# Adjacency times features on one core: main groups of five row tiles in place of four

## The chip, the cores and the metric

The kernel runs on one core of a Trainium2 chip. The metric is the device time of one execution in microseconds; the kernel before takes 638.62 us (median of 3 runs, 638.38 to 640.05).

## The reference

`x` is 8192 x 64, `adj` is 8192 x 8192, both float32. What is computed:

```
agg = adj @ (x @ W_agg)
y   = w[:, None] * relu(agg) + (1 - w)[:, None] * x
out = layernorm(x + y)            # over the 64 columns, eps 1e-5, no scale or shift
```

The adjacency matrix is 268.4 MB and is read once; everything else is small.

## The kernel before

The product is taken in the order (adj @ x) @ W_agg. The 8192 nodes are 64 tiles of 128 rows of the output, and 64 tiles of 128 source nodes. An adjacency tile is stored transposed and packed on the host, so that one row of a load (one SBUF partition) holds, for a run of source tiles, the columns of several row tiles side by side. TensorE holds a tile of `x` (128 x 64) as weights and streams the adjacency; the 64 x columns sums are gathered in PSUM. Even source tiles write PSUM partitions 0 to 63, odd ones 64 to 127 (`into[j % 2 * D:...]`), so two neighbouring matmuls use different halves of the array. `aggT` then holds the sums of both halves, and a second matmul with `wagg2` (W_agg twice, one over the other) turns them into rows and adds the halves.

The row tiles come in three stages: main, 60 row tiles in G = 15 groups of `MAIN_SLOTS` = 4 (512 columns); mid, 3 row tiles (384 columns); last, 1 row tile (128 columns).

- Loads (SyncE, lines 105 to 137). A main group comes in three loads of `MAIN_LOADS` = 22, 22 and 20 source tiles; row c of the ring is a slot of 22 x 512 columns (44 KB in a partition, 132 KB for three). A load's rows are 45,056 or 40,960 bytes, 128 of them. Load c of the next group waits until TensorE has finished slot c (`slot_free`). Mid (8 loads, L130) and last (9 loads, L136) reuse the same ring behind the last main group. The rows 0 to 62 of the output tiles are stored by SyncE (L141) when mid is normalised, the last one by ScalarE (L214).
- TensorE (L144 to L187). In a hardware loop over the groups: for each load wait for `loaded[c]`, then `contract` (L156), one matmul for each source tile; the profile shows each float32 matmul as two records of LDWEIGHTS and two of MATMUL. Then `turn_back` (L164), four matmuls of 64 columns with 128 x 128 weights, behind the wait for ScalarE's copy. After the loop the same for mid and last, written out.
- ScalarE (L203) copies the sums of a group from PSUM into `aggT` when all three loads are contracted, and takes square roots (L199).
- VectorE (L230 to L267): relu, weight, residual and layer norm of a group from `rows_ps`, seven short steps.

One DMA queue (SyncE's) carries all loads in program order, and each engine's work is in program order too.

Of the kernel before, what the change touches and what calls it, by code (L numbers as in the profile page):

```python
# [4 lines left out]
P = 128  # L5
D = 64
EPS = 1e-5
HALVES = 1
MAIN_SLOTS = 4
MID_SLOTS = 3  # L10
LAST_SLOTS = 1
SUB = 64
MAIN_LOADS = (22, 22, 20)
# [4 lines left out]
def gnn_residual_layernorm(nc, x, adj_main, adj_mid, adj_last, w, w_agg, out):  # L18
# [15 lines left out]
    T = x.shape[0] // P  # L34
    G = adj_main.shape[0]
    MID, LAST = G, G + 1
    MID_T0 = G * MAIN_SLOTS
    LAST_T0 = MID_T0 + MID_SLOTS
    COLS, MID_COLS = MAIN_SLOTS * P, MID_SLOTS * P
    C = len(MAIN_LOADS)  # L40
    SLOT = max(MAIN_LOADS) * COLS
    LAST_AT = T * MID_COLS
    assert SUB == T == sum(MAIN_LOADS) == sum(MID_LOADS) == sum(LAST_LOADS) and LAST_T0 + LAST_SLOTS == T
    assert LAST_AT + T * P <= C * SLOT and LAST_AT > (C - 1) * SLOT


    DVE_PRE = 2
# [5 lines left out]
    with ctx:  # L53
        def sb(name, shape):
            return ctx.enter_context(nc.sbuf_tensor(name, shape, fp32))

        def psum(name, shape):
            return ctx.enter_context(nc.psum_tensor(name, shape, fp32))

        def sem(name):  # L60
            return ctx.enter_context(nc.semaphore(name))

        ring = sb("ring", [P, C * SLOT])
        x_sb = sb("x_sb", [P, T, D])
# [5 lines left out]
        aggT = sb("aggT", [P, COLS])  # L70
        y = sb("y", [P, MAIN_SLOTS, D])
        sq = sb("sq", [P, MAIN_SLOTS, D])
        rowsum = sb("rowsum", [P, MAIN_SLOTS])
        varsum = sb("varsum", [P, MAIN_SLOTS])
        std = sb("std", [P, MAIN_SLOTS])
# [5 lines left out]
        mv = sb("mv", [P, 2])  # L81

        bank = psum("bank", [P, 8, 512])
        acc = bank[:, 0]
        mid_acc = bank[:, 1, 0:MID_COLS]
        last_acc = bank[:, 2, 0:P]
        rows_ps = bank[:, 3, 0:MAIN_SLOTS * D]
        mid_rows = bank[:, 4, 0:MID_SLOTS * D]
        last_rows = bank[:, 5, 0:D]

        loaded = [sem(f"loaded{c}") for c in range(C)]
        mid_loaded = [sem(f"mid_loaded{k}") for k in range(len(MID_LOADS))]
# [1 line left out]
        slot_free = sem("slot_free")  # L94
# [3 lines left out]
        agg_copied = sem("agg_copied")  # L98
# [8 lines left out]
        @block.sync  # L107
        def _(sp):
            sp.dma_start(x_sb[:], x.rearrange("(p t) d -> p t d", p=P)).then_inc(x_in, 16)  # L109
            sp.dma_start(w_sb[:], w.rearrange("(p t) -> p t", p=P)).then_inc(w_in, 16)  # L110
            def main_load(c, load):

                j, n = sum(MAIN_LOADS[:c]), MAIN_LOADS[c]
                sp.dma_start(ring[:, c * SLOT:c * SLOT + n * COLS], load[:, :, j:j + n].rearrange("o q s n -> (o q) (s n)")  # L114
                             ).then_inc(loaded[c], 16)

            for c in range(C):
                main_load(c, adj_main[0:1, 0])
            with sp.Fori(1, G) as g:
                for c in range(C):  # L120

                    sp.wait_ge(slot_free, g * C + (c + 1 - C))
                    main_load(c, adj_main[bass.ds(g, 1), 0])

            j, freed = 0, 0
            for k, n in enumerate(MID_LOADS):
                while freed * SLOT < (j + n) * MID_COLS:
                    freed += 1
                    sp.wait_ge(slot_free, (G - 1) * C + freed)
                sp.dma_start(ring[:, j * MID_COLS:(j + n) * MID_COLS],  # L130
                             adj_mid[0, :, j:j + n].rearrange("q s n -> q (s n)")).then_inc(mid_loaded[k], 16)
                j += n
            sp.wait_ge(slot_free, G * C)
            j = 0
            for k, n in enumerate(LAST_LOADS):
                sp.dma_start(ring[:, LAST_AT + j * P:LAST_AT + (j + n) * P],  # L136
                             adj_last[:, j:j + n].rearrange("q s n -> q (s n)")).then_inc(last_loaded[k], 16)
                j += n

            sp.wait_ge(out_ready, LAST)  # L140
            sp.dma_start(out_rows[:, 0:LAST_T0], res[:, 0:LAST_T0]).then_inc(stored, 16)  # L141
# [5 lines left out]
        @block.tensor  # L147
        def _(pe):
            pe.wait_ge(x_in, 16)
            pe.wait_ge(wagg_in, 32)  # L150

            def contract(into, at, cols, j0, n):

                for s in range(n):
                    j = j0 + s
                    last = nc.tensor.matmul(into[j % 2 * D:(j % 2 + 1) * D, 0:cols], x_sb[:, j],  # L156
                                            ring[:, at + s * cols:at + (s + 1) * cols], start=j < 2, stop=j >= T - 2)
                return last

            def turn_back(rows, n, copied):  # L160

                pe.wait_ge(agg_copied, copied)
                for i in range(n):
                    last = nc.tensor.matmul(rows[:, i * D:(i + 1) * D], aggT[:, i * P:(i + 1) * P], wagg2[:], start=True, stop=True)  # L164
                last.then_inc(rows_done, 1)

            with pe.Fori(0, G) as g:
                for c in range(C):
                    pe.wait_ge(loaded[c], g * 16 + 16)
                    contract(acc, c * SLOT, COLS, sum(MAIN_LOADS[:c]), MAIN_LOADS[c]).then_inc(slot_free, 1)  # L170

                pe.wait_ge(dve_step, g * DVE_GROUP + DVE_PRE)
                turn_back(rows_ps, MAIN_SLOTS, g + 1)
            j = 0
            for k, n in enumerate(MID_LOADS):
                pe.wait_ge(mid_loaded[k], 16)
                last = contract(mid_acc, j * MID_COLS, MID_COLS, j, n)
                j += n
            last.then_inc(mid_done, 1)
            turn_back(mid_rows, MID_SLOTS, MID + 1)  # L180
            j = 0
            for k, n in enumerate(LAST_LOADS):
                pe.wait_ge(last_loaded[k], 16)
                last = contract(last_acc, LAST_AT + j * P, P, j, n)
                j += n
            last.then_inc(last_done, 1)
            turn_back(last_rows, LAST_SLOTS, LAST + 1)  # L187

        @block.scalar
        def _(act):  # L190
            for h in range(2):
                act.dma_start(wagg2[h * D:(h + 1) * D, :], w_agg).then_inc(wagg_in, 16)

            nc.scalar.preload_act_table_set("sqrt_and_others")  # L194
            act.wait_ge(eps_ready, 1)

            def std_of(out_std, var, scale, var_step):
                act.wait_ge(dve_step, var_step)
                nc.scalar.activation(out_std, var, ACT.Sqrt, bias=eps[:, 0:1], scale=scale).then_inc(std_ready, 1)  # L199

            with act.Fori(0, G) as g:
                act.wait_ge(slot_free, g * C + C)
                nc.scalar.copy(aggT[:], acc).then_inc(agg_copied, 1)  # L203
                std_of(std[:], varsum[:], 1.0 / D, g * DVE_GROUP + (DVE_PRE + VAR_STEP))

                act.wait_ge(out_ready, g + 1)
            act.wait_ge(mid_done, 1)
            nc.scalar.copy(aggT[:, 0:MID_COLS], mid_acc).then_inc(agg_copied, 1)  # L208
            std_of(std[:, 0:MID_SLOTS], varsum[:, 0:MID_SLOTS], 1.0 / D, MID * DVE_GROUP + (DVE_PRE + VAR_STEP))
            act.wait_ge(last_done, 1)  # L210
            nc.scalar.copy(aggT[:, 0:P], last_acc).then_inc(agg_copied, 1)  # L211
            std_of(std_last[:], mv[:, 1:2], 1.0, LAST_STEP0 + LAST_VAR_STEP)
            act.wait_ge(out_ready, LAST + 1)
            act.dma_start(out_rows[:, LAST_T0:T], res[:, LAST_T0:T]).then_inc(stored, 16)  # L214
            act.wait_ge(stored, 2 * 16)
# [85 lines left out]
```

## Time and profile before

| | before |
|---|---|
| time, median of 3 runs | 638.62 us (638.38 to 640.05) |
| time of the profiled execution | 638.89 us |
| its span, first to last instruction | 637.0 us |
| TensorE matmul busy | 519.5 us (82%) |
| VectorE busy | 55.8 us (9%) |
| ScalarE busy | 15.9 us (2%) |
| DMA queue of SyncE, share of 16 DMA engines | 99.6% |
| moved | 272.75 MB, mean 428 GB/s |
| mean granted TensorE clock | 0.912 |

The time of an execution is 1.9 us longer than its span. Busy times are unions: an engine with two operations at once counts once. "Idle before" is time in which an engine had nothing running, with what ended it.

### The profile page before, as it was taken

The page shows a single profiled execution, that of the slowest core. Times are in us where ns is not written, and L with a number is a line of the kernel's source. Part 1 is how long each engine was busy: PE and PEld are TensorE (multiplying, and loading weights), DVE is VectorE, ACT ScalarE, POOL GpSimd, SP SyncE. Part 2 cuts the span into 40 slices and gives each one's busy share as a digit, 9 for nine tenths or more (in the row PEclk, how much of TensorE's full clock was granted, in tenths as well). Part 3 has the DMA queues.
Part 4 walks back from the last instruction along what each step waited for, and adds up shares of the span by engine and source line. Part 5 has one row for each costly group of instructions (what it writes and reads, how often), then busy time and mean ns, then how long its engine had stood idle before and what let it go on. Part 6 is the DMA issues. An engine that isn't in the chain of part 4 may idle for free.

```text
span 637.0 us, 5371 instructions
## 1 busy us (share of the span) xinstructions
PE 519.5 (82%) x2304; PEld 177.2 (28%) x2304; DVE 55.8 (9%) x136; ACT 15.9 (2%) x35; POOL 0.3 (0%) x5
## 2 busy tenths in 40 slices
PE   0678798878987888797878977878887987978996
PEld 0123232222222322222222322322222222222345
DVE  2000101010010100101001010100101001010102
ACT  0000000000000000000000000000000000000000
POOL 0000000000000000000000000000000000000000
PEclk9997898888979889897988979898888989888999
DMA  9999999999999999999999999999999999999998
GB/s 362 453 418 453 419 427 433 425 447 428 444 414 447 419 429 443 441 432 419 451 410 436 436 450 423 427 431 425 446 424 453 424 429 419 436 444 420 428 413 349
DMA packets 9667, 272.75 MB, mean 428 GB/s; under 512 B 1472, under 2 KB 1728, under 8 KB 3008
## 3 DMA queue, kind: packets, MB, share of 16 engines
q1 hardware_dynamic: 9360, 272.63, 99.6%
q10 hardware_dynamic: 304, 0.07, 0.1%
q8 instruction: 3, 0.05, 0.0%
HBM read 270.60 MB, written 2.10 MB: 428 GB/s over the span
## 4 chain that ended last, share of the span: by engine, by line
DMA 69%; PE 29%; issue 0%; SPq 0%; ACT 0%; DVE 0%; DVEq 0%
DMA ring<-adj_main_dram 69%; PE bank L156 29%; PE bank L164 0%; SPq L114 0%; ACT aggT L203 0%; ACT aggT L208 0%; SPq L110 0%; SPq L109 0%; DVE res L267 0%; ACT std_last L199 0%; DVE y_last L261 0%; ACT aggT L211 0%; DVE stats L263 0%; DVE y_last L262 0%; DVE mv L264 0%
## 5 line engine op out<-in xcount | busy, mean ns | idle before, releaser
L156 PE MATMUL bank<-ring,x_sb 128*64 128x512 f32 (+2 forms) x2176 | 501.7, 621 | 102.2 <-DMA ring<-adj_main_dram 102.1
L156 PEld LDWEIGHTS bank<-ring,x_sb 128*64 128x64 f32 x2176 | 161.6, 148 | 430.2 <-issue 299.7
L245 DVE SCALAR_TENSOR_TENSOR y<-bank,w_sb 128x256 f32<-128x256 f32 (+1 forms) x16 | 6.7, 420 | 552.7 <-PE bank L164 552.7
L164 PE MATMUL bank<-wagg,aggT 128*128 128x64 f32 x128 | 17.9, 281 | 11.2 <-ACT aggT L203 10.3
L164 PEld LDWEIGHTS bank<-wagg,aggT 128*128 128x128 f32 x128 | 15.6, 191 | 25.4 <-ACT aggT L203 23.5
L203 ACT COPY aggT<-bank 128x512 f32<-128x512 f32 x15 | 8.8, 585 | 527.0 <-PE bank L156 527.0
L234 DVE TENSOR_TENSOR y<-y,res 128x256 f32<-128x256 f32 (+1 forms) x16 | 6.7, 420 | 2.2
L242 DVE TENSOR_TENSOR res<-y,rstd 128x256 f32 (+1 forms) x16 | 6.7, 421 | 0.6
L238 DVE TENSOR_TENSOR sq<-y 128x256 f32<-128x256 f32 (+1 forms) x16 | 6.7, 421 | 0.6
L236 DVE SCALAR_TENSOR_TENSOR y<-rowsum,y 128x256 f32<-128x256 f32 (+1 forms) x16 | 6.7, 420 | 0.5
L239 DVE TENSOR_REDUCE varsum<-sq 128x4 f32<-128x256 f32 (+1 forms) x16 | 6.7, 416 | 0.5
L235 DVE TENSOR_REDUCE rowsum<-y 128x4 f32<-128x256 f32 (+1 forms) x16 | 6.6, 416 | 0.6
L199 ACT ACTIVATE std<-varsum,eps 128x4 f32<-128x4 f32 (+1 forms) x16 | 4.8, 297 | 65.7 <-DVE varsum L239 65.7
L230 DVE TENSOR_TENSOR res<-x_sb,two_minus_w 128x4096 f32<-128x4096 f32 x1 | 4.4, 4425 | 0.0
L241 DVE RECIPROCAL rstd<-std 128x4 f32<-128x4 f32 (+1 forms) x16 | 2.8, 178 | 6.9 <-ACT std L199 6.9
L194 ACT ACT_TABLE_LOAD x1 | 1.3, 1283 | 2.0 <-issue 2.0
L227 DVE TENSOR_SCALAR two_minus_w<-w_sb 128x64 f32<-128x64 f32 x1 | 0.2, 194 | 9.2 <-DMA w_sb<-w_dram 9.2
L208 ACT COPY aggT<-bank 128x384 f32<-128x384 f32 x1 | 0.5, 478 | 17.5 <-PE bank L156 17.5
L261 DVE TENSOR_SCALAR y_last<-bank,w_sb 128x64 f32<-128x64 f32 x1 | 0.3, 284 | 4.8 <-PE bank L164 4.8
L211 ACT COPY aggT<-bank 128x128 f32<-128x128 f32 x1 | 0.3, 265 | 4.7 <-PE bank L156 4.7
L199 ACT ACTIVATE std_last<-mv,eps 128x1 f32<-128x1 f32 x1 | 0.3, 296 | 1.6 <-DVE mv L264 1.6
L267 DVE TENSOR_SCALAR res<-y_last,mv,rstd_last 128x64 f32<-128x64 f32 x1 | 0.3, 314 | 0.0
(9 smaller groups left out, 1.3 us busy)
## 6 DMA issues: line engine op xcount, KB each, us to landing
ring<-adj_main_dram SPq DMA_DIRECT2D x30, 5632.0 KB, 27.2
ring<-adj_main_dram SPq DMA_DIRECT2D x15, 5120.0 KB, 29.8
ring<-adj_mid_dram SPq DMA_DIRECT2D x2, 2304.0 KB, 22.8
ring<-adj_mid_dram SPq DMA_DIRECT2D x1, 3072.0 KB, 21.5
ring<-adj_mid_dram SPq DMA_DIRECT2D x2, 1536.0 KB, 23.9
x_sb<-x_dram SPq DMA_DIRECT2D x1, 2048.0 KB, 8.0
out_dram<-res SPq DMA_DIRECT2D x1, 2016.0 KB, 8.1
ring<-adj_last_dram SPq DMA_DIRECT2D x2, 768.0 KB, 23.0
```

What stands on the lines that cost most here:

```text
L156: last = nc.tensor.matmul(into[j % 2 * D:(j % 2 + 1) * D, 0:cols], x_sb[:, j], ring[:, at + s * cols:at + (s + 1) * cols], start=j < 2, st ...
L164: last = nc.tensor.matmul(rows[:, i * D:(i + 1) * D], aggT[:, i * P:(i + 1) * P], wagg2[:], start=True, stop=True)
L199: nc.scalar.activation(out_std, var, ACT.Sqrt, bias=eps[:, 0:1], scale=scale).then_inc(std_ready, 1)
L203: nc.scalar.copy(aggT[:], acc).then_inc(agg_copied, 1)
L230: step(nc.vector.tensor_tensor(res[:], x_sb[:], over_row(two_minus_w[:]), ALU.mult), DVE_PRE)
L234: step(nc.vector.tensor_tensor(v, v, residual, ALU.add), base + 2)
L235: step(nc.vector.tensor_reduce(rowsum[:, 0:n], v, AX.X, ALU.add), base + 3)
L236: step(nc.vector.scalar_tensor_tensor(out=v, in0=over_row(rowsum[:, 0:n]), scalar=-1.0 / D, in1=v, op0=ALU.mult, op1=ALU.add), base + 4)
L238: step(nc.vector.tensor_tensor(s, v, v, ALU.mult), base + 5)
L239: step(nc.vector.tensor_reduce(varsum[:, 0:n], s, AX.X, ALU.add), base + VAR_STEP)
L242: nc.vector.tensor_tensor(residual, v, over_row(rstd[:, 0:n]), ALU.mult).then_inc(out_ready, 1)
L245: step(nc.vector.scalar_tensor_tensor(out=y[:, 0:n], in0=rows.rearrange("p (n d) -> p n d", d=D), scalar=0.0, in1=over_row(w_sb[:, bass.ds ...
```

## The change

`MAIN_SLOTS` goes from 4 to 5: twelve main groups in place of fifteen, each of 640 columns. The source tiles of the three loads stay 22, 22 and 20, so the rows of a load grow to 56,320 and 51,200 bytes and the ring to 165 KB. 640 float32 columns do not fit one PSUM bank of 512, so the sums of a group lie in two (`acc` with 512 columns, `acc_rest` with 128), and each source tile takes two matmuls. They are issued for two source tiles at a time: even and odd tile into `acc`, then even and odd tile into `acc_rest`. ScalarE copies the two banks one after the other, and `turn_back` has five matmuls. Mid and last are as before, in other banks. The counts awaited on `agg_copied` follow from two copies in each group. The bytes moved and the multiply-adds are the same.

```diff
-MAIN_SLOTS = 4
+MAIN_SLOTS = 5
...
-    assert LAST_AT + T * P <= C * SLOT and LAST_AT > (C - 1) * SLOT
+    assert LAST_AT + T * P <= C * SLOT and all(n % 2 == 0 for n in MAIN_LOADS)
...
-        acc = bank[:, 0]
-        mid_acc = bank[:, 1, 0:MID_COLS]
-        last_acc = bank[:, 2, 0:P]
-        rows_ps = bank[:, 3, 0:MAIN_SLOTS * D]
-        mid_rows = bank[:, 4, 0:MID_SLOTS * D]
-        last_rows = bank[:, 5, 0:D]
+        BANK = bank.shape[2]
+        acc, acc_rest = bank[:, 0], bank[:, 1, 0:COLS - BANK]
+        mid_acc = bank[:, 2, 0:MID_COLS]
+        last_acc = bank[:, 3, 0:P]
+        rows_ps = bank[:, 4, 0:MAIN_SLOTS * D]
+        mid_rows = bank[:, 5, 0:MID_SLOTS * D]
+        last_rows = bank[:, 6, 0:D]
...
+            def contract_main(c):
+
+                for s in range(0, MAIN_LOADS[c], 2):
+                    for into, c0, c1 in (acc, 0, BANK), (acc_rest, BANK, COLS):
+                        for half in range(2):
+                            j, at = sum(MAIN_LOADS[:c]) + s + half, c * SLOT + (s + half) * COLS
+                            last = nc.tensor.matmul(into[half * D:(half + 1) * D], x_sb[:, j], ring[:, at + c0:at + c1],
+                                                    start=j < 2, stop=j >= T - 2)
+                return last
+
...
-                    contract(acc, c * SLOT, COLS, sum(MAIN_LOADS[:c]), MAIN_LOADS[c]).then_inc(slot_free, 1)
+                    contract_main(c).then_inc(slot_free, 1)
 
                 pe.wait_ge(dve_step, g * DVE_GROUP + DVE_PRE)
-                turn_back(rows_ps, MAIN_SLOTS, g + 1)
+                turn_back(rows_ps, MAIN_SLOTS, g * 2 + 2)
...
-                nc.scalar.copy(aggT[:], acc).then_inc(agg_copied, 1)
+                nc.scalar.copy(aggT[:, 0:BANK], acc).then_inc(agg_copied, 1)
+                nc.scalar.copy(aggT[:, BANK:COLS], acc_rest).then_inc(agg_copied, 1)
```

## Rows read from the trace of the kernel before

**Rows 1.** The page's DMA queues: packets, MB, share of the 16 engines' span.

```profile
q1 hardware_dynamic: 9360, 272.63, 99.6%
q8 instruction: 3, 0.05, 0.0%
```

**Rows 2.** TensorE's timeline, two groups: start us, us, operation, idle before and its end.

```profile
126.51 8.80 PE L156 MATMUL bank<-ring,x_sb 128*64 128x512 f32 x40 [0.76 <-DMA ring<-adj_main_dram]
136.00 1.10 PE L164 MATMUL bank<-wagg,aggT 128*128 128x64 f32 x8 [0.69 <-ACT aggT L203]
139.84 11.21 PE L156 MATMUL bank<-ring,x_sb 128*64 128x512 f32 x44 [2.73 <-DMA ring<-adj_main_dram]
153.18 11.36 PE L156 MATMUL bank<-ring,x_sb 128*64 128x512 f32 x44 [2.14 <-DMA ring<-adj_main_dram]
165.30 8.80 PE L156 MATMUL bank<-ring,x_sb 128*64 128x512 f32 x40 [0.76 <-DMA ring<-adj_main_dram]
```

**Rows 3.** The chain that ended last, from the last main load: start us, us, what.

```profile
562.14 29.77 DMA ring<-adj_main_dram
591.91 0.04 issue
591.95 8.83 PE bank L156 x40
600.78 0.02 issue
600.80 0.59 ACT aggT L203
...
602.55 20.82 PE bank L156 x128
```

**Rows 4.** TensorE's timeline, from the mid stage to the end.

```profile
623.92 0.88 PE L164 MATMUL bank<-wagg,aggT 128*128 128x64 f32 x6 [0.58 <-ACT aggT L208]
624.73 7.38 PE L156 MATMUL bank<-ring,x_sb 128*64 128x128 f32 x128
```

**Rows 5.** The issue of the smallest loads of the last stage, and the page's line for them.

```profile
617.46 0.79 SPq L136 DMA_DIRECT2D ring<-adj_last_dram  x1
...
ring<-adj_last_dram SPq DMA_DIRECT2D x2, 128.0 KB, 14.4
```

**Rows 6.** DMA totals from 100 to 560 us with the queue's line, and from 621 to 629.

```profile
DMA packets 5121, 199.17 MB, mean 433 GB/s; under 512 B 561, under 2 KB 561, under 8 KB 561
q1 hardware_dynamic: 5121, 199.17, 100.3%
...
DMA packets 937, 3.25 MB, mean 406 GB/s; under 512 B 100, under 2 KB 210, under 8 KB 937
```

**Rows 7.** TensorE's timeline, first microseconds of the last stage, and of last main load.

```profile
624.73 2.19 PE L156 MATMUL bank<-ring,x_sb 128*64 128x128 f32 x36
624.73 5.02 PE L156 MATMUL bank<-ring,x_sb 128*64 128x128 f32 x88
...
591.95 0.20 PEld L156 LDWEIGHTS bank<-ring,x_sb 128*64 128x64 f32 x4 [1.65 <-DMA ring<-adj_main_dram]
592.43 0.14 PEld L156 LDWEIGHTS bank<-ring,x_sb 128*64 128x64 f32 x2 [0.29 <-issue]
592.86 0.14 PEld L156 LDWEIGHTS bank<-ring,x_sb 128*64 128x64 f32 x2 [0.29 <-issue]
```

**Rows 8.** ScalarE's copy of 128 columns, by form: busy us, mean ns, idle before.

```profile
L211 ACT COPY aggT<-bank 128x128 f32<-128x128 f32 x1 | 0.3, 265 | 4.7 <-PE bank L156 4.7
```

**Rows 9.** TensorE's timeline, first group, and DMA queues from 42 to 47 us.

```profile
35.36 9.66 PE L156 MATMUL bank<-ring,x_sb 128*64 128x512 f32 x44 [1.25 <-DMA ring<-adj_main_dram]
48.95 11.41 PE L156 MATMUL bank<-ring,x_sb 128*64 128x512 f32 x40 [3.92 <-DMA ring<-adj_main_dram]
...
q1 hardware_dynamic: 75, 2.52, 117.4%
q8 instruction: 1, 0.02, 1.4%
```

**Rows 10.** Third loads: the chain; timeline; two stretches with busy us, granted clock, DMA share, GB/s.

```profile
126.51 8.83 PE bank L156 x40
...
514.38 10.53 PE bank L156 x40
...
204.09 10.50 PE L156 MATMUL bank<-ring,x_sb 128*64 128x512 f32 x40 [2.46 <-DMA ring<-adj_main_dram]
...
204.00:214.70 10.70, 10.50 (x40) 3.18 (x40) 0.84 0.94 404
591.90:600.80 8.90, 8.80 (x40) 2.78 (x40) 1.00 0.99 423
```

More of the change, by code:

```diff
@@ L179, in _ @@
             last.then_inc(mid_done, 1)
-            turn_back(mid_rows, MID_SLOTS, MID + 1)
+            turn_back(mid_rows, MID_SLOTS, G * 2 + 1)
             j = 0
@@ L186, in _ @@
             last.then_inc(last_done, 1)
-            turn_back(last_rows, LAST_SLOTS, LAST + 1)
+            turn_back(last_rows, LAST_SLOTS, G * 2 + 2)
         @block.scalar
```

## The prediction

> **What bounds the kernel now.** I read four views in this order. The page's DMA queues come first: SyncE's queue fills 99.6% of the 16 engines' span [rows 1]. So the stream of loads sets the pace, and a main group takes what its bytes take: the third loads of two neighbouring groups are met by TensorE at 126.51 and 165.30 us, 38.79 us apart [rows 2]. In TensorE's timeline every load of a group is waited for, with 0.76, 2.73 and 2.14 us of idle time [rows 2]. There TensorE has slack, and what it does more costs nothing as long as the slot comes free before the two other loads in the queue have landed; they last over 25 us, TensorE needs 9 to 12.
>
> The third view is the chain from the last main load on. It lands at 591.91 us, and from there the chain is TensorE without a wait for data: 8.83 us of contraction, ScalarE's copy of 0.59 us, `turn_back`, 20.82 us of mid [rows 3]. In this stretch the slack is gone, because mid and last carry fewer columns for each source tile and TensorE is about as slow as the stream. The fourth view, the timeline of the end, tells how near the two are. The last loads land at about 617.46 + 14.4 = 631.9 us [rows 5]; TensorE finishes at 624.73 + 7.38 = 632.11 [rows 4]. How long would it take if nothing held it? The first 36 records of the last stage take 2.19 us and the first 88 take 5.02 [rows 7]. They run two by two, so 26 pairs take 2.83 us, 0.109 us each, and the 20 pairs up to 128 records would take 2.18 more: 7.20 us. The row has 7.38. The data hold TensorE up by only 0.18 us: at the end of the kernel both bound it, within 0.2 us. Whatever makes TensorE later between the last main landing and the end shows up in full, and whatever makes the stream faster helps only through the landing of that last main load.
>
> **The change, part by part.**
>
> *The stream.* Bytes are the same, rows fewer: each of the 16 engines carries 8 of the 128 rows of a load, so 15 groups x 3 x 8 = 360 main rows become 12 x 3 x 8 = 288, 72 fewer. What a row costs beyond its bytes comes from two stretches [rows 6]. From 100 to 560 us: 5121 - 561 = 4560 rows, 43.7 KB each (199.17 MB by 4560), 460 us x 16 / 4560 = 1614 ns a row. From 621 to 629 us: 837 rows of 3.88 KB, 8 x 16 / 837 = 153 ns. The slope is 1461 ns for 39.8 KB, 36.7 ns a KB; what remains is 153 - 143 = 10 ns a row. 72 x 10 ns = 0.7 us less. Bounds: nothing, and 1.1 us were it 15 ns. I take -0.7 us for the landing of the last main load.
>
> *Contraction of the last main load.* 20 source tiles get a second matmul of 128 columns. The last stage shows just such matmuls at 0.109 us for a pair of records [rows 7]; 20 tiles have 40 records, 20 pairs: 20 x 0.109 = +2.2 us. Bounds: nothing (short steps wholly beside long ones, G below), and +5.4 (F below); I take the step of the row, since it is the same shape, back to back. In the same load the 512-column part stays at 8.8 us. In all other main loads the same kind of time (22 x 0.11 = 2.4 us) lies in the wait for the next load, which grows with it: a stream of 13.3 us for 44 KB rows becomes 16.7 us.
>
> *ScalarE.* A second copy, of 128 columns, behind the first: 0.265 us [rows 8] plus a little issue, +0.3 us. TensorE's `turn_back` waits for both, and mid is queued behind it.
>
> *turn_back.* 8 records take 1.10 us, 6 take 0.88 [rows 2, 4]; two more cost +0.22 us.
>
> *VectorE.* 320 columns in place of 256 in seven steps of a group; nobody waits for a main group's result before the store at the end, and mid's own steps are unchanged: nothing. *SyncE:* 9 loads fewer to issue, mid's loads are freed earlier; nothing, since the queue is full. Three fewer loop turns hide in TensorE's idle time.
>
> *Sum.* TensorE's path behind the last main landing grows by 2.2 + 0.3 + 0.22 = 2.7 us; the 0.18 us in which it was held up is used up by it: +2.5. The landing is 0.7 earlier: +1.8 us. The final store starts that much later as well. The profiled execution took 638.89 us, so 640.7 on its scale; it lies 0.27 us above the median of 638.62, so **640.4 us**. Its own range is 639.7 to 641.3 (the row cost from 1.1 to 0 us, and 0.1 or 0.2 us for the copy and the changes between shapes). A measurement of this kernel can tell about 0.3%, 1.9 us, from no change: the forecast is just below that.
>
> **The rivals.**
>
> *B, slower: the last main load meets the lower clock.* In 8 of the 13 third loads that stand by themselves in the chain TensorE needs 8.83 us, the first at 126.51, the last at 591.95 [rows 3, 10]; in 5 about 10.5 us, the first at 204.09, the last at 514.38 [rows 10]. At 204.09 the granted clock of the stretch is 0.84 in place of 1.00 [rows 10], part of it at 1.2 in place of 2.4 GHz. That one comes behind a longer idle time, 2.46 us against 0.76 for the fast ones shown [rows 2, 10]. With the change the second load takes 2.4 us more and the stream between second and third grows by 3.0, so the idle time is about 0.6 us longer: 1.4 or 3.1 us. The price is the 1.7 us of the rows, now fully on the path: 642.1 us. It decides as soon as the last third load starts at the low clock.
>
> *C, earlier: code.* Between 42 and 47 us one packet of instructions comes in (0.02 MB) [rows 9], and the third load of the first group takes 13.59 us from landing to landing (35.36 to 48.95) in place of the 12.12 of 153.18 to 165.30 [rows 2, 9]. 1.47 us are lost there on one DMA engine and never come back. The changed loop body has 64 more matmuls, so such packets come at other moments and perhaps on other engines. If none falls on the latest engine: 638.9 us. *D:* one more falls there: 641.9.
>
> *E: the loop body no longer stays in the instruction memory.* Between 100 and 560 us all 5121 packets are SyncE's loads [rows 6], none is code, though the loop turns 12 times. Were the larger body fetched anew at each of the 11 returns, and each time at 1.5 us on the deciding engine, it would be +16.5, 656.9 us. The Trainium skill (Runtime: NRT & Kernel Launch, Instruction fetch mechanics) has the rule that a taken branch out of a window of two 16 KiB pages forces a fetch, and gives TensorE 128 KiB of instruction memory; by the first this change would pay, by the second not. No row here shows a body of this size.
>
> *F: short and long matmuls don't pair.* Before, two records start together at every step, from the first weights of a load on (4 weight loads in 0.20 us, then 2 in every 0.43) [rows 7]. If records kept strict program order (both of the even tile, then both of the odd one), a pair of tiles would take three long steps and a short one, 3 x 0.43 + 0.11 = 1.40 us, in place of 2 x 0.43 + 2 x 0.11 = 1.08: +3.2 us over 10 pairs, 643.6. Against it speaks the common start of the first two. The Trainium skill (TensorE: Matmul & The Clock Gate, Part 3, The mechanism) says that matmuls start and end in program order; that rule would favour F.
>
> *G, faster: the stream alone decides.* If the short matmuls cost nearly nothing beside the long ones, the end follows the stream, -0.7 us, 637.9; with C, 636.4.
>
> **How the numbers follow.** Forecast 0.48 (within 0.3% 0.27, slower 0.21), B 0.20, C 0.12 (0.11 within, 0.01 faster), D 0.06, E 0.03, F 0.04, G 0.07 (0.03 within, 0.04 faster). Slower: 0.21 + 0.20 + 0.06 + 0.03 + 0.04 = 0.54. Within: 0.27 + 0.11 + 0.03 = 0.41. Faster: 0.05. The range 638.3 to 642.8 holds the forecast, B, C and D, 0.86 less their edges; E, F and G lie mostly outside.
>
> **What would show it.** In the changed profile: third loads 48.3 to 48.5 us apart (38.79 x 1.25 less 0.2); the last main load landing near 591.2 us and contracted in about 11.0 us; two ScalarE copies, 0.9 us together; mid starting near 604.3 in place of 602.5; mid at 20.8 us; the last stage without any wait, 7.2 us. B shows as a last contraction over 12.5 us, C and D as the landing moved by 1.5 us, E as instruction packets in every group, F as 14 us. The prediction is wrong if TensorE waits for data in the last stage again.

## The result and the profile after

The changed kernel takes 640.31 us (median of 16 runs, 639.81 to 642.02), the kernel before in runs beside it 639.15 us (16 runs, 638.38 to 640.27). The ratio is 1.0022 with a 95% interval of 1.0013 to 1.0031: 0.2% slower, less than the 0.3% that the prediction took as its bound. 640.4 us had been forecast.

The times of both kernels lie in two clusters. Before: 8 runs from 638.4 to 638.9 us and 8 from 639.4 to 640.3. After: 11 runs from 639.8 to 640.4 and 5 from 641.7 to 642.0. Lower cluster against lower cluster (638.75 and 640.22, their medians) the change costs 1.5 us. Both profiled executions are of the lower one.

| | before | after |
|---|---|---|
| profiled execution / span | 638.89 / 637.0 us | 640.43 / 638.5 us |
| TensorE matmul busy | 519.5 us | 508.7 us |
| last main load landed | 591.91 us | 591.22 us |
| its contraction | 8.83 us | 11.01 us |
| start of mid | 602.48 us | 604.36 us |
| last stage | 624.73 + 7.38 us | 626.61 + 7.21 us |

The queues of the changed kernel on its page (packets, MB, share of the 16 engines) are those of [rows 1] with 1296 packets fewer, and one more of instructions:

```profile
q1 hardware_dynamic: 8064, 272.63, 99.2%
q10 hardware_dynamic: 304, 0.07, 0.0%
q8 instruction: 4, 0.07, 0.0%
```

The chain of the changed kernel, two neighbouring third loads and then the stretch behind the last one (start us, us, what), answers to [rows 2, 3]:

```profile
494.37 0.04 issue
494.42 11.01 PE bank L167 x80
...
542.80 0.04 issue
542.84 12.70 PE bank L167 x80
...
591.22 0.04 issue
591.26 11.01 PE bank L167 x80
602.27 0.02 issue
602.29 0.04 ACT aggT L214
602.34 0.44 issue
602.78 0.28 ACT aggT L215
603.06 0.04 issue
603.10 1.33 PE bank L175 x10
604.43 20.82 PE bank L157 x128
```

Third loads land 48.43 us apart, 542.80 to 591.22 among them. From the last one on there is again no wait for data, and each piece of TensorE's path that the change touches is longer. The second copy (L215) begins at 602.78 us, 0.10 us before the first one (602.29 + 0.59) ends, so the chain shows only a part of the first. TensorE's timeline of the end, which answers to [rows 4], shows the last stage without its hold:

```profile
625.80 0.88 PE L175 MATMUL bank<-wagg,aggT 128*128 128x64 f32 x6 [0.58 <-ACT aggT L220]
626.61 7.21 PE L157 MATMUL bank<-ring,x_sb 128*64 128x128 f32 x128
```

### The profile page after: what moved, and what is told of

Same layout as the page of the kernel before. It is cut to its first block, busy times and chain, and to the rows that moved or that the text cites. A ratio compares the mean times of both kernels' runs of the same rounds, so it can differ in the third digit from the quotient of the medians.

```text
span 638.5 us, 7549 instructions
## 1 busy us (share of the span) xinstructions
PE 508.7 (80%) x3456; PEld 239.1 (37%) x3456; DVE 52.2 (8%) x112; ACT 15.3 (2%) x41; POOL 0.3 (0%) x5
## 4 chain that ended last, share of the span: by engine, by line
DMA 70%; PE 29%; issue 0%; SPq 0%; DVE 0%; ACT 0%; another core or an unknown queue 0%; DVEq 0%
DMA ring<-adj_main_dram 70%; PE bank L167 24%; PE bank L157 4%; PE bank L175 0%; SPq L115 0%; ACT aggT L220 0%; SPq L111 0%; SPq L110 0%; DVE res L279 0%; ACT std_last L210 0%; DVE y_last L273 0%; ACT aggT L215 0%; ACT aggT L223 0%; DVE stats L275 0%
## 5 line engine op out<-in xcount | busy, mean ns | idle before, releaser
L167 PE MATMUL bank<-ring,x_sb 128*64 128x512 f32 (+1 forms) x3072 | 463.5, 465 | 114.8 <-DMA ring<-adj_main_dram 114.8
L167 PEld LDWEIGHTS bank<-ring,x_sb 128*64 128x64 f32 x3072 | 207.7, 146 | 369.2 <-issue 247.1
L257 DVE SCALAR_TENSOR_TENSOR y<-bank,w_sb 128x320 f32<-128x320 f32 (+1 forms) x13 | 6.3, 481 | 560.3 <-PE bank L175 560.3
L157 PE MATMUL bank<-ring,x_sb 128*64 128x384 f32 (+1 forms) x256 | 28.1, 380 | 0.0
L157 PEld LDWEIGHTS bank<-ring,x_sb 128*64 128x64 f32 x256 | 16.1, 137 | 11.2 <-issue 11.1
L246 DVE TENSOR_TENSOR y<-y,res 128x320 f32<-128x320 f32 (+1 forms) x13 | 6.3, 482 | 1.7
L254 DVE TENSOR_TENSOR res<-y,rstd 128x320 f32 (+1 forms) x13 | 6.3, 483 | 0.4
L248 DVE SCALAR_TENSOR_TENSOR y<-rowsum,y 128x320 f32<-128x320 f32 (+1 forms) x13 | 6.3, 483 | 0.4
L250 DVE TENSOR_TENSOR sq<-y 128x320 f32<-128x320 f32 (+1 forms) x13 | 6.3, 481 | 0.4
L247 DVE TENSOR_REDUCE rowsum<-y 128x5 f32<-128x320 f32 (+1 forms) x13 | 6.2, 478 | 0.4
L251 DVE TENSOR_REDUCE varsum<-sq 128x5 f32<-128x320 f32 (+1 forms) x13 | 6.2, 477 | 0.4
L215 ACT COPY aggT<-bank 128x128 f32<-128x128 f32 x12 | 3.3, 271 | 0.0
```

The source lines that it names most:

```text
L167: last = nc.tensor.matmul(into[half * D:(half + 1) * D], x_sb[:, j], ring[:, at + c0:at + c1], start=j < 2, stop=j >= T - 2)
L246: step(nc.vector.tensor_tensor(v, v, residual, ALU.add), base + 2)
L247: step(nc.vector.tensor_reduce(rowsum[:, 0:n], v, AX.X, ALU.add), base + 3)
L248: step(nc.vector.scalar_tensor_tensor(out=v, in0=over_row(rowsum[:, 0:n]), scalar=-1.0 / D, in1=v, op0=ALU.mult, op1=ALU.add), base + 4)
L250: step(nc.vector.tensor_tensor(s, v, v, ALU.mult), base + 5)
L251: step(nc.vector.tensor_reduce(varsum[:, 0:n], s, AX.X, ALU.add), base + VAR_STEP)
```

## The experiments

**What sets the end.** Two theories stood: TensorE's work behind the last main landing, or something else that five row tiles bring with them (start-up, copies, queue). The first experiment leaves the 128-column matmuls of every third load out, all but those of its last pair of source tiles; a part of the sums is then missing.

```diff
-                    for into, c0, c1 in (acc, 0, BANK), (acc_rest, BANK, COLS):
+                    for into, c0, c1 in ((acc, 0, BANK), (acc_rest, BANK, COLS))[:1 if c == C - 1 and s < MAIN_LOADS[c] - 2 else 2]:
```

> The 128-column matmuls of the third load are left out in every group but for the last pair of source tiles, so that part of the sums of one row tile in five is missing. Theory (TensorE's work behind the last main landing sets the end): 9 pairs x 0.218 us = 2.0 us less there, lower cluster at 638.3 us (changed kernel 640.2 less 2.0, of which the data give back nothing since TensorE's end would be 631.9 us and the data allow 631.5). Rival (the 1.7 us come from something else: the start-up, the copies, the queue): no change, 640.2 us.

Measured: median 639.55 us over 10 runs, five from 638.35 to 638.85 and five from 640.24 to 640.62. On the same chip the changed kernel's lower cluster lay at 640.39 (below), 1.6 us higher, where 2.0 had been expected. TensorE's timeline of the third contraction and of the last stage:

```profile
591.13 9.02 PE L167 MATMUL bank<-ring,x_sb 128*64 128x512 f32 x44 [1.39 <-DMA ring<-adj_main_dram]
624.52 7.21 PE L157 MATMUL bank<-ring,x_sb 128*64 128x128 f32 x128
```

The contraction is 1.97 us shorter (10.99 less 9.02), the load is met within 0.2 us of the same time, and the last stage starts 2.09 us earlier than at 626.61, without a hold. So the work behind the landing does set the end of the changed kernel. The profiled execution (638.51 us) is 1.9 us below the first one of the changed kernel and 2.0 below the one of the same chip; the clusters' medians (638.81 and 640.39) differ by 0.4 less, and why is open. The upper cluster stays, at 640.43 us in five of ten runs.

**The two clusters.** Theory: in the upper one the last third load is contracted partly at 1.2 GHz, as some third loads of earlier groups are. Loads of 24, 22 and 18 source tiles shorten the third contraction, and the shorter stream between the second and the third load leaves less idle time before it; the ring is packed for it.

```diff
-MAIN_LOADS = (22, 22, 20)
+MAIN_LOADS = (24, 22, 18)
...
-    SLOT = max(MAIN_LOADS) * COLS
+    AT = [sum(MAIN_LOADS[:c]) * COLS for c in range(C + 1)]
...
-                sp.dma_start(ring[:, c * SLOT:c * SLOT + n * COLS], load[:, :, j:j + n].rearrange("o q s n -> (o q) (s n)")
+                sp.dma_start(ring[:, AT[c]:AT[c] + n * COLS], load[:, :, j:j + n].rearrange("o q s n -> (o q) (s n)")
```

> Loads of 24, 22 and 18 source tiles in place of 22, 22 and 20, packed without gaps in the ring; rows 61,440, 56,320 and 46,080 bytes, as many rows as before the edit. Theory: the third contraction has one pair less, 1.08 us, so the lower cluster falls from 640.2 to 639.1 us; and since the stream between second and third landing (13.6 us) is about as long as the second contraction (11.9 at full clock, 13.6 with its slow start), TensorE has at most 1.8 us idle before the third load and starts it at full clock: the upper cluster is gone. Rival (the clusters don't come from the clock): the upper cluster stays at +1.7 us in a third of the runs.

Measured: 639.14 us, ten runs from 638.87 to 639.47, 1.25 us below the lower cluster of the changed kernel on the same chip (1.1 expected), and there is no upper cluster. TensorE's timeline has the last third contraction at 9.91 us, behind a landing at the same time:

```profile
577.64 12.06 PE L167 MATMUL bank<-ring,x_sb 128*64 128x512 f32 x88 [1.28 <-DMA ring<-adj_main_dram]
591.27 9.91 PE L167 MATMUL bank<-ring,x_sb 128*64 128x512 f32 x72 [1.56 <-DMA ring<-adj_main_dram]
```

The changed kernel was then timed again, and three single executions were profiled, two of it and one of the kernel before, to meet one of the upper cluster:

> The changed kernel once more, beside the kernels below. Theory: times in two clusters, 640.1 to 640.4 us and about 1.7 us above, 641.7 to 642.0, the upper one in about a third of the runs (the last main load contracted partly at 1.2 GHz). If the two clusters had another cause (a late landing), the landing of the last main load would differ between runs and not the contraction behind it.

> The changed kernel, one execution with its profile, to meet an execution of the upper cluster (about three in ten). If its time is above 641.5 us, theory: the last main load lands at 591.2 us as before, and its contraction takes about 12.7 us in place of 11.0, at a granted clock below 1.00. Rival: the landing itself is about 1.7 us late and the contraction takes 11.0.

> The same once more: in an execution above 641.5 us the last contraction takes about 12.7 us behind a landing at 591.2 us; in one of the lower cluster 11.0 us behind the same landing.

> The kernel before, one execution with its profile. If its time is above 639.4 us (half of its runs), theory: landing of the last main load at 591.9 us, contraction 10.5 us in place of 8.8, and of the 1.7 us the 0.2 in which TensorE was held up by data are taken off: the end is 1.3 to 1.5 us later. Below 639.1: contraction 8.8 us.

The changed kernel once more, timed over 8 runs: six from 639.92 to 640.61 us (median 640.39), two at 641.77 and 642.01. The single executions took 640.34, 640.22 and (kernel before) 638.82 us, so each was of a lower cluster, and the profiles show it so: landings at 591.1 to 591.2 (591.9 before), contractions of 10.99 (8.80). What they add is that the landing and the full-clock contraction repeat within 0.1 us. An upper execution itself was not met, so the cause of the upper cluster is not shown directly. That it is the clock is argued from three things. The first is the price, which is that of a slow third load in the same trace. The two stretches of the changed kernel, last and last but one group (busy us of the contraction, granted clock, DMA share, GB/s), answer to [rows 10]:

```profile
591.20:602.30 11.10, 10.99 (x80) 5.04 (x80) 1.00 1.00 428
542.80:555.60 12.80, 12.68 (x80) 5.77 (x80) 0.87 1.01 436
```

1.69 us more at a clock of 0.87: part of that stretch ran at 1.2 in place of 2.4 GHz. The clusters are 1.7 us apart (641.90 and 640.22, medians). For the kernel before the distance is 1.2 us (639.97 and 638.75), where a slow third load less the hold would give 1.5.

The second is the share. If any group, the last one too, can meet the lower clock, then the share of slow third loads in the profiles should be about the share of upper runs. It is, with every run of a kernel counted, those beside other kernels too:

| | slow third loads in the profiles | runs in the upper cluster |
|---|---|---|
| kernel before (2 profiles) | 12 of 30 | 25 of 63 |
| changed kernel (4 profiles) | 12 of 48 | 7 of 26 |
| without the short matmuls of third loads | 5 of 12 | 5 of 10 |
| loads of 24, 22 and 18 | 0 of 12 | 0 of 10 |

The third is that the upper cluster goes away together with the long waits. In the four profiles of the changed kernel a third load waits about 3.07 us or at most 1.54 us; all twelve slow ones (12.68 us) are among the fourteen that waited 3.07. With loads of 24, 22 and 18 every third load waits 1.4 to 1.6 us and no slow one is left. The upper cluster is gone as well where TensorE's path no longer sets the end (the finer ends below). TensorE's timeline of the changed kernel has all three kinds, start us, us, operation, wait:

```profile
252.34 12.68 PE L167 MATMUL bank<-ring,x_sb 128*64 128x512 f32 x80 [3.08 <-DMA ring<-adj_main_dram]
446.00 10.99 PE L167 MATMUL bank<-ring,x_sb 128*64 128x512 f32 x80 [1.39 <-DMA ring<-adj_main_dram]
494.42 10.99 PE L167 MATMUL bank<-ring,x_sb 128*64 128x512 f32 x80 [3.07 <-DMA ring<-adj_main_dram]
```

The mean granted clock of a whole run does not settle it. It is 0.915 in both clusters of the kernel before where it was listed; in the kernel without those short matmuls it is 0.902 in the lower and 0.899 in the upper one. So the clock is the likely cause in both kernels, and a profile of an upper execution would decide.

**The stream by itself.** If the longer rows shorten the stream, that must show where TensorE no longer decides. So the last group is written out behind the loop, its second load comes in 12 and 10 source tiles and its third in 14 and 6, each awaited by itself, on both kernels. The edit on the changed kernel:

```diff
+FINAL_PARTS = ((22,), (12, 10), (14, 6))
...
-            with sp.Fori(1, G) as g:
+            with sp.Fori(1, G - 1) as g:
...
+            for c in range(C):
+                sp.wait_ge(slot_free, (G - 1) * C + (c + 1 - C))
+                k, load = 0, adj_main[G - 1:G, 0]
+                for i, m in enumerate(FINAL_PARTS[c]):
+                    j = sum(MAIN_LOADS[:c]) + k
+                    sp.dma_start(ring[:, c * SLOT + k * COLS:c * SLOT + (k + m) * COLS],
+                                 load[:, :, j:j + m].rearrange("o q s n -> (o q) (s n)")).then_inc(final_loaded[c][i], 16)
+                    k += m
...
+            for c in range(C):
+                s0 = 0
+                for i, m in enumerate(FINAL_PARTS[c]):
+                    pe.wait_ge(final_loaded[c][i], 16)
+                    last = contract_main(c, s0, m)
+                    s0 += m
+                last.then_inc(slot_free, 1)
```

> The changed kernel with the last of its twelve groups written out behind the loop, its second load in two transfers of 12 and 10 source tiles and its third in two of 14 and 6, each awaited by itself. Theory (the work behind the last landings sets the end, and the clock falls in the waits before them): TensorE no longer waits for a whole load, its contraction of the last group ends about 599.5 us and the end follows the data again: 16 rows more on each engine, +0.16 us, against 0.7 us less of stream: 0.5 us below the lower cluster of the kernel before, and no upper cluster. Rival (the stream was not shortened by longer rows): level with the lower cluster of the kernel before or above it. Rival (code written out costs its fetches on the latest DMA engine): 1.5 us or 3 us above that.

> The same edit on the kernel before: four row tiles, last of fifteen groups written out, its loads in the same parts. Theory: the end was bound by the data already, so the lower cluster stays within 0.2 us of that of the kernel before, and its upper cluster (about 1.2 us higher, half of the runs) is gone. The difference between this kernel and the one above with five row tiles is then the stream alone: 72 rows x 10 ns = 0.7 us. Rival (a row costs nothing of its own): difference 0.

Measured: with five row tiles 638.32 us (11 runs, 638.08 to 638.48), ratio to the kernel before 0.9988 (0.9979 to 0.9998); with four 638.82 us (11 runs, 638.67 to 638.93), ratio 0.9996 (0.9987 to 1.0005). No upper cluster in either. The first is 0.12% below the kernel before, and 0.39 us below the lower cluster of its runs on this chip (638.71); it is 0.3% below the changed kernel, which was timed on other chips. TensorE's timeline of the end with five row tiles:

```profile
586.66 10.99 PE L177 MATMUL bank<-ring,x_sb 128*64 128x512 f32 x80 [3.57 <-DMA ring<-adj_main_dram]
599.82 9.25 PE L167 MATMUL bank<-ring,x_sb 128*64 128x384 f32 x56
609.55 6.67 PE L167 MATMUL bank<-ring,x_sb 128*64 128x384 f32 x40 [0.47 <-DMA ring<-adj_mid_dram]
616.94 5.38 PE L167 MATMUL bank<-ring,x_sb 128*64 128x384 f32 x32 [0.72 <-DMA ring<-adj_mid_dram]
623.71 7.69 PE L167 MATMUL bank<-ring,x_sb 128*64 128x128 f32 x128
```

The third contraction begins at 586.66 us, 4.6 us earlier than at 591.26; mid now waits for its data, and the last stage takes 7.69 us in place of 7.21 since data hold it. The end follows the stream, and there the five-tile kernel is 0.50 us faster than the four-tile one. 0.7 had been expected. One thing was not held equal: the five-tile kernel fetches six packets of code and the four-tile one four. One of the two that it has more comes between 540 and 580 us, in the written-out part; whether it costs anything was not measured.

The cost of a row was then taken in the other direction: the kernel before with each main load in two transfers, so that the number of main rows doubles.

```diff
-                sp.dma_start(ring[:, c * SLOT:c * SLOT + n * COLS], load[:, :, j:j + n].rearrange("o q s n -> (o q) (s n)")
-                             ).then_inc(loaded[c], 16)
+                for k in (0, n // 2):
+                    sp.dma_start(ring[:, c * SLOT + k * COLS:c * SLOT + (k + n // 2) * COLS],
+                                 load[:, :, j + k:j + k + n // 2].rearrange("o q s n -> (o q) (s n)")).then_inc(loaded[c], 16)
...
-                    pe.wait_ge(loaded[c], g * 16 + 16)
+                    pe.wait_ge(loaded[c], g * 32 + 32)
```

> The kernel before with each main load in two transfers of half its source tiles, both awaited together: rows of 22,528 and 20,480 bytes, 360 more of them on each DMA engine. Theory (10 ns a row beyond its bytes): 360 x 10 = 3.6 us longer, groups 39.02 us apart in place of 38.78, lower cluster 642.3 us. With 15 ns a row it would be 5.4 us (644.1), with none no change (638.7).

Measured: 642.63 us over 4 runs, two at 642.00 and 642.17, two at 643.10 and 643.44; ratio 1.0061 (1.0045 to 1.0076). The chain's third loads:

```profile
556.23 10.38 PE bank L157 x40
595.25 8.83 PE bank L157 x40
```

39.02 us apart in place of 38.79. The last is met 3.30 us later than at 591.95 [rows 3]: 3.30 us by the 360 additional rows of each DMA engine is 9.2 ns a row, what a second transfer costs by itself included.

**The order of the matmuls.** The change issues even and odd source tile into one bank before it goes to the other. The same matmuls tile by tile:

```diff
-                    for into, c0, c1 in (acc, 0, BANK), (acc_rest, BANK, COLS):
-                        for half in range(2):
+                    for half in range(2):
+                        for into, c0, c1 in (acc, 0, BANK), (acc_rest, BANK, COLS):
```

> Only the order of the matmuls: for each source tile its 512 and then its 128 columns, in place of even and odd tile into one bank and then into the other. Theory (a matmul is started in program order and holds its half of the array for both of its steps): the odd tile's 512 columns wait until the even tile's 128 have been started, which is at the end of its 512; a pair of tiles takes 4 x 0.43 = 1.72 us in place of 1.08, a group 32 x 1.72 + 2.8 = 57.8 us against 48.4 us of stream, and the kernel is bound by TensorE: 25 + 12 x 57.8 + 37 = 756 us. Rival (the halves run freely, each with its own order): 640 to 642 us, no change.

Measured: 640.39 us in one run, no change. TensorE's timeline has the last contraction in 11.04 us:

```profile
591.28 11.04 PE L167 MATMUL bank<-ring,x_sb 128*64 128x512 f32 x80 [1.35 <-DMA ring<-adj_main_dram]
```

My theory fell: the odd tile's matmul does not wait for the even tile's short one. How far, then, may the matmuls of the two halves stand apart in the program? Two more orders, blocks of four source tiles with the even ones first, and a whole load with the even ones first:

```diff
+                n = MAIN_LOADS[c]
+                for s, half in [(s, half) for b in range(0, n, 4) for half in range(2) for s in range(b, min(b + 4, n), 2)]:
...
```

> Order alone: in each block of four source tiles first both even ones with their 512 and 128 columns, then both odd ones, so that four matmuls of one half stand ahead of the first of the other. If the halves run freely whatever stands between (what the order by tile suggests): 640 to 642 us. If TensorE looks only some matmuls ahead, fewer than four: a block takes up to 3.9 us in place of 2.15, and the kernel is bound by TensorE at up to 25 + 12 x 65.2 + 37 = 844 us.

> Order alone: in each load first all even source tiles, then all odd ones, 20 or 22 matmuls of one half ahead of the other. If the halves run freely whatever stands between: 640 to 642 us. If the look ahead ends before 20 matmuls, much of each load is contracted with one half at a time: up to 64 x 1.08 = 69 us a group against 48.4 us of stream, and up to 25 + 12 x 71.8 + 37 = 924 us.

Measured: 641.73 and 858.28 us, one run each. 641.73 lies near the upper cluster, but its trace shows another cause. In blocks of four TensorE's timeline has the last contraction in 12.57 us in place of 10.99:

```profile
591.00 12.57 PE L168 MATMUL bank<-ring,x_sb 128*64 128x512 f32 x80 [1.49 <-DMA ring<-adj_main_dram]
```

The granted clock of the stretch is 1.00, so that is the order's price, 1.6 us more; in all groups but the last it hides in the wait for the next load. By whole loads TensorE bounds the kernel. Its timeline in the middle of a load, and the changed kernel's:

```profile
404.73 6.62 PE L168 MATMUL bank<-ring,x_sb 128*64 128x128 f32 x24
```

```profile
591.74 3.83 PE L167 MATMUL bank<-ring,x_sb 128*64 128x512 f32 x26
```

24 records in 6.6 us against 26 in 3.8: nearly the time of one half after the other. In 1.94 us around the place where the even tiles end there are more than that:

```profile
402.52 1.94 PE L168 MATMUL bank<-ring,x_sb 128*64 128x128 f32 x11
```

11 records, where one half alone would have 7 or 8. So the halves do run together there, for about one source tile, and not over a distance of 20 matmuls.

## Why the prediction was right

*The bound.* Right. Every main load is still waited for, the last one by 0.51 us in this trace: the group line of the main contraction in the changed profile (busy, mean ns, idle before) has 114.8 us of waits, before 102.1, so the 2.4 us more of every first and second load cost nothing. Only behind the last landing is there no next load to hide in.

```profile
L167 PE MATMUL bank<-ring,x_sb 128*64 128x512 f32 (+1 forms) x3072 | 463.5, 465 | 114.8 <-DMA ring<-adj_main_dram 114.8
```

The end was bound within 0.2 us by both sides, and after the change by TensorE alone: 7.21 us for the last stage where 7.20 had been worked out for an unheld one.

*The stream, -0.7 us.* Landing 591.22 for 591.91: -0.69. It builds up over the groups: from 107.08 to 591.26 us a group takes 48.42 us, where five quarters of the former one (38.79) are 48.49. Where it decides by itself it gave 0.50 us, and from the doubled rows a row costs 9.2 ns for the 10 of the sum. Both are inside the bounds.

*The third contraction, +2.2 us.* 11.01 for 8.83: +2.18. The step of 0.109 us from the last stage holds beside long matmuls too.

*The copies, +0.3 us.* From the end of the contraction to the end of the second copy it is now 0.79 us (602.27 to 603.06), before 0.62 for one (600.78 to the next matmul's issue at 601.40). This term was put too high: 0.17 and not 0.3, since the second copy starts before the first has ended.

*turn_back, +0.22 us.* 1.33 for 1.10: +0.23.

*The hold, -0.18.* 7.38 to 7.21: 0.17. The sum by the trace is -0.69 + 2.18 + 0.17 + 0.23 - 0.17 = +1.72; TensorE ends the last stage at 633.82 us for 632.11, +1.71. The span grew by 1.5 us only, the lower cluster by 1.47: the small last store was finished 0.2 us sooner behind the last instruction of VectorE. Together with the copies that makes the 0.3 us between the growth that was forecast (1.8) and that of the lower cluster.

*What was luck.* Each term came out near its size, but 640.4 against 640.31 us is closer than the forecast was. It had 1.8 us of growth on 638.62, a median of three runs that lies in the lower cluster. The growth was 1.47 us from lower cluster to lower cluster and 1.16 us between the medians, because the median of before fell between its clusters, at 639.15. A base 0.5 us too low and a growth 0.6 us too high cancel to 0.1 us.

*The rivals.* B's time came in part: 5 of 16 runs are 1.7 us above the others, and the idle times that it worked out, 1.4 or 3.1 us, are those of the trace (1.38 and 3.07). That its clock is the cause in those runs is likely and not shown. As a share of single runs 0.20 was a little low. What I had not drawn from the three times of before (640.05 beside 638.62 and 638.38) is that two clusters were to be seen there already: half of its 16 runs are in the upper one. C and D did not happen. TensorE's timeline of the first groups, and the queues from 36 to 75 us, answer to [rows 9]:

```profile
25.43 13.50 PE L167 MATMUL bank<-ring,x_sb 128*64 128x512 f32 x88 [25.43 <-DMA ring<-adj_main_dram]
43.52 14.68 PE L167 MATMUL bank<-ring,x_sb 128*64 128x512 f32 x88 [4.59 <-DMA ring<-adj_main_dram]
...
75.32 14.15 PE L167 MATMUL bank<-ring,x_sb 128*64 128x512 f32 x88 [3.48 <-DMA ring<-adj_main_dram]
91.97 13.76 PE L167 MATMUL bank<-ring,x_sb 128*64 128x512 f32 x88 [2.50 <-DMA ring<-adj_main_dram]
...
q1 hardware_dynamic: 359, 16.86, 100.2%
q8 instruction: 2, 0.03, 0.4%
```

Two packets of code come in this stretch, one between 38 and 40 us and one between 60 and 75. The second load lands 18.09 us after the first where 75.32 to 91.97 has 16.65: 1.44 us are lost, where the kernel before loses 1.47 with its packet; from there to 75.32 there are 31.80 us for a third and a first load (15.13 + 16.65 = 31.78), so the other packet cost nothing. That the first packet is what costs the 1.44 us fits in time in both kernels, and no run tests it. E did not happen: between 76 and 600 us the DMA totals have SyncE's loads alone.

```profile
DMA packets 4810, 226.56 MB, mean 432 GB/s; under 512 B 528, under 2 KB 528, under 8 KB 528
## 3 DMA queue, kind: packets, MB, share of 16 engines
q1 hardware_dynamic: 4810, 226.56, 100.0%
```

The loop body of 133 matmuls has 532 records of weights and matmuls, by the 256 instructions to 16 KiB of the Trainium skill (Runtime: NRT & Kernel Launch, Instruction fetch mechanics) an estimate of 33 KiB. By the same section's rule its branch back should have left a window of two 16 KiB pages, by 1 KiB only if each record is one instruction, and forced a fetch; the trace doesn't show one. It fits the same section's larger memory for TensorE. F did not happen either, and the order by tile goes further than the trace of the change. The Trainium skill's rule that matmuls start in program order (TensorE: Matmul & The Clock Gate, Part 3, The mechanism) would have made that order slow, and the trace shows the last contraction at 11.04 us. G did not happen: the short matmuls cost their full step.

*The gain that was there to be had.* The stream did get shorter, by 0.5 to 0.7 us. More than three times that (2.4 us) was given back on TensorE's path behind the last main landing, because the last load of a group grew with the group. With finer loads in the last group alone the gain shows: 638.32 us, against 638.82 for four row tiles with the same finer loads.

## What to carry to other kernels

A stream that fills the DMA engines sets the middle of a kernel, but its end is set by the work behind the last large landing; when a tile grows, price that work first, and make the last loads small. Where two limits end within a few tenths of a microsecond, work out from its steps how long the last stage would take if no data held it, and compare that with its row: the difference tells how much slack is left. And look at all the times of a kernel, not at the median alone. Two clusters with the distance of a stall that the trace shows elsewhere are a reason to count it: how many of the groups have the stall, and how many of the runs lie in the upper cluster.

## What the runs showed of the hardware

- Two halves of the array run side by side without strict program order between them. With two matmuls of one half ahead of the other nothing is lost (last contraction 11.04 us), with four a little (12.57), and with 20 or 22 most of the overlap (kernel 858 us).
- A row of a large transfer costs 9 to 10 ns beyond its bytes: 9.2 ns when rows of 41 and 45 KB are halved, what the second transfer costs included, and an estimate of 10 ns from the rows of the kernel before [rows 6].
- A long wait does not always bring the lower clock: the kernel with the finer end waits 3.57 us before its last contraction and then runs it in 10.99 us, at a granted clock of 1.00. In four profiles of the changed kernel twelve of fourteen third loads that waited about 3.07 us were slow and two were not.
